# TensorE's instruction order beside a chain of scans: the shared expert's pieces dealt 5 in 8 slots, router and projection queued later

## The reference

```
xc, z = split(x @ W_in.T)                       # 256 + 256
xs = silu(conv3(xc))                            # three taps along time
dt = softplus((xs @ W_x[:64].T) @ W_dt.T + b_dt) + 1e-5
B, Cp = xs @ W_x[64:80].T, xs @ W_x[80:].T      # 16 + 16 per token
s_t = exp(-exp(A_log) * dt_t) * s_(t-1) + B_t * dt_t * xs_t     # state: 256 x 16
y = (Cp @ W_C.T) * sum_n(s_t) + D * xs
layer 1: x1 = x + layernorm((y @ W_out.T) * silu(z)),   fed with layernorm(x)
layer 2, on xn = layernorm(x1):
    router: softmax(xn @ gate_w.T), the best 2 of 8 experts, weights normalised
    routed = sum over the 2 experts of w_e * (gelu(xn @ W1_e + b1_e) @ W2_e + b2_e)   # 256 -> 1024 -> 256
    shared = gelu(xn @ sW1 + sb1) @ sW2 + sb2                                          # 256 -> 1024 -> 256
    out = x1 + layernorm(routed + shared)
```

## Time and profile before

| | us |
|---|---|
| median of 3 runs | 1368.14 |
| the profiled execution | 1368.64 |
| its span, first to last instruction | 1366.8 |
| chunks 0 to 7, first scan to last scan | 47.41 to 632.28 |
| tail to the last router logit | 632.28 to 678.66 |

### The profile page before, as it was taken

The page is one execution under the profiler, slowest core; times in us unless marked ns, Lnnn a source line. Parts: engine busy times, 40 slices in busy tenths (PEclk is TensorE's granted clock), DMA queues, the critical chain, the costliest instruction groups (busy, mean ns, idle before and its releaser), DMA issues.

```text
span 1366.8 us, 14546 instructions
## 1 busy us (share of the span) xinstructions
PE 1142.7 (84%) x4810; PEld 902.0 (66%) x4810; DVE 699.8 (51%) x1201; ACT 625.4 (46%) x1129; POOL 594.5 (43%) x637
## 2 busy tenths in 40 slices
PE   4445597877969697849578999999999999999996
PEld 2112274655637373637577888888888888888874
DVE  1699999899989989895365111111111111111126
ACT  4683977777877887845130221222212222122212
POOL 2594958677695948663001232322323223232111
PEclk9676699897979798878795999999999999999998
DMA  4100102011010101010104365766677656456456
GB/s 136 32 0 0 47 1 75 3 47 31 24 54 24 54 1 62 0 56 7 62 5 161 96 225 174 255 205 226 215 241 247 214 165 221 175 190 214 138 169 200
DMA packets 117835, 152.18 MB, mean 111 GB/s; under 512 B 15206, under 2 KB 102591, under 8 KB 117760
## 3 DMA queue, kind: packets, MB, share of 16 engines
q1 hardware_dynamic: 110272, 132.63, 29.9%
q0 software_dynamic: 7488, 18.63, 3.7%
HBM read 126.06 MB, written 27.00 MB: 112 GB/s over the span
## 4 chain that ended last, share of the span: by engine, by line
PE 58%; DVE 14%; POOL 9%; issue 8%; ACT 8%; DMA 1%; SPq 1%; DVEq 0%; POOLq 0%; ACTq 0%
PE psum L728 20%; PE psum L740 20%; PE psum L672 6%; POOL Ssum L1269 5%; DVE S L907 5%; PE psum L662 2%; PE psum L700 2%; DVE psum L888 2%; PE psum L687 2%; ACT A L1166 2%; DVE stats L843 2%; PE psum L769 1%; PE psum L715 1%; PE psum L642 1%; POOL xs L1243 1%
## 5 line engine op out<-in xcount | busy, mean ns | idle before, releaser
L1208 ACT ACTIVATE h<-psum,bb 128x256 f32<-128x256 f32 x312 | 130.7, 470 | 475.7 <-PE psum L728 444.7
L1269 POOL TENSOR_TENSOR Ssum<-Ssum,S 128x512 f32<-128x512 f32 x240 | 302.3, 1267 | 75.3 <-DVE S L907 75.2
L728 PE MATMUL psum<-XT,w 128*128 128x256 f32 x1248 | 278.8, 382 | 0.9 <-DVE XT L1021 0.9
L740 PE MATMUL psum<-w,h 128*128 128x256 f32 x1248 | 275.8, 379 | 0.0
L728 PEld LDWEIGHTS psum<-XT,w 128*128 128x128 f32 x1248 | 239.1, 192 | 34.4 <-DVE XT L1021 1.3
L740 PEld LDWEIGHTS psum<-w,h 128*128 128x128 f32 x1248 | 234.2, 190 | 30.3
L1294 POOL DMA_INDIRECT z_d<-y,ids x78 | 78.4, 1005 | 390.2 <-DVE y L1029 376.5
L1166 ACT ACTIVATE A<-dts,nea 128x512 f32<-128x512 f32 x256 | 177.3, 720 | 23.0 <-DVE S L907 19.8
L888 DVE TENSOR_TENSOR psum<-us,psum 128x512 f32<-128x512 f32 x256 | 163.6, 683 | 26.2 <-PE psum L628 24.2
L1029 DVE TENSOR_TENSOR y<-bb,psum 128x256 f32<-128x256 f32 x78 | 29.3, 417 | 249.3 <-PE psum L740 249.3
L1021 DVE COPY XT<-psum 128x512 f32<-128x512 f32 x39 | 27.0, 691 | 246.9 <-PE psum L715 240.7
(11 more groups left out here) (153 smaller groups left out, 1196.1 us busy)
## 6 DMA issues: line engine op xcount, KB each, us to landing
w<-W SPq DMA_DIRECT2D x78, 1024.0 KB
Z<-z_d SPq DMA_DIRECT2D x32, 256.0 KB, 6.7
bb<-b SPq DMA_DIRECT2D x39, 128.0 KB
xnb<-x SPq DMA_DIRECT2D x16, 256.0 KB, 3.7
Xr<-x SPq DMA_DIRECT2D x16, 256.0 KB, 3.1
x_d<-gb SPq DMA_DIRECT2D x8, 512.0 KB, 2.9
xn_d<-nb SPq DMA_DIRECT2D x8, 512.0 KB, 3.2
sh_d<-O SPq DMA_DIRECT2D x16, 256.0 KB, 2.5
```

The source lines that it names most:

```text
L728: i = eng.matmul(PS[3 + m % 3][:, 256 * ff:256 * ff + 256], w1[n % 2][:, k, 128 * (f + ff):128 * (f + ff) + 128], xT[n % 2][:, k, :], star ...
L740: i = eng.matmul(PS[6 + n % 2][:, 256 * j:256 * j + 256], h[n % 2][:, f, 128 * j:128 * j + 128], w2[n % 2][:, f, :], start=f == 0, stop=f ...
L1208: eng.activation(h[n % 2][:, f + ff, :], PS[3 + m % 3][:, 256 * ff:256 * ff + 256], ACT.Gelu, bias=bb1[n % 2][:, f + ff:f + ff + 1]).then_ ...
L1269: eng.tensor_tensor(to, to, of, ALU.add).then_inc(nsum, 1)
```

## The change

`shared` is advanced in slots where `5 * k % 8 < 5` only, which are 5 of every 8, instead of in all of them; `post` is stretched over slots 2 to 29 instead of 2 to 27, and gets one more empty step before norm 3 and two between the `nT` copies and `logit`; `prep` gets one more empty step between `silu` and `dtc`. No instruction is added or removed. All lines behind the edits are 6 higher in the changed kernel (628 is 634).

```
-FIRST_POST, LAST_POST, LAST_PREP = 2, 27, 26
+FIRST_POST, LAST_POST, LAST_PREP = 2, 29, 26
...
         say("silu", i)
+        yield
         yield
         yield
         d, p, t0, t1 = (next(use) for _ in range(4))
...
         if not late:
             yield
             yield
+            yield
         yield from normalised(3, i, late)
         say("store_xn", i)
         yield from crossed("nT", i)
+        if not late:
+            yield
+            yield
         g = next(use)
         say("logit", i, g)
...
-            if i:
+
+            if i and 5 * k % 8 < 5:
                 part(beside, 1)
```

## The result

The changed kernel takes 1390.72 us (median of 4 runs, 1390.43 to 1391.23) against 1367.92 for the kernel before in the same comparison: a ratio of 1.0165 with a 95% interval of 1.0147 to 1.0183. It is slower by 22.8 us. The forecast was 1367.3 us, and its range ended at 1377.

What follows compares the result with a forecast made beforehand. DVE was taken to set the pace, its idle waits being winnable. Chunks 2 to 6 +2.1, chunk 1 -4.0, chunk 7 -0.5, tail +1.6: -0.8 on 1368.64, less 0.5 to the median, 1367.3 us; eight-in-ten range 1353 to 1377.

Steps and rivals of the forecast that it cites:

- The gelu block of 5.39 us in front of decay 15: Slot 10's gelu and table loads behind norm 2 delay decays: DVE waits 2.9 us at slot 15, 1.8 at slot 19.
- the late waits behind the logit and the `s1` pieces: DVE's waits for spreads 14 and 15 go, as both spreads now stand ahead of that PE work; part of 21.9 us.
- GpSimd's 4.7 us: DVE's waits for the residual in chunks 2 to 6 go, as it now precedes the second convolution in GpSimd's queue.
- The tail: After the last chunk, `Xr` loads later behind the last `s2_out`, so the residual starts at 667.8 instead of 666.23: +1.6 us.
- Rival 1: Slot 10's gelu is covered by ACT's idling, so no scan waits for a decay: 1345 us, chance 0.14.
- Rival 3: The logit still waits for `nT` copies that come later, so the change fails its purpose: +7, 1375 us, chance 0.08.
- All 21.9 us go.: In chunks 2 to 6, all of `mult`'s waits for spreads, 21.9 us in 20 waits, disappear.
- rival 2: PE's half clock holds through slots 18 to 23 (`dtc`, `s2`, `bp`), making spread 11 late: +15, 1382 us, chance 0.10.
- the size of `gated`'s wait: `gated` of the second half, now behind slot 7 instead of 8, waits for the second `wout`: 0.6 us per chunk.
- the rule on gaps that the prediction weighed: Skill's advice: short matmul bursts with idle gaps fall to half clock, so keep them together; its effect was put as rival 2.
- Chunk 1: No gelu in slot 10 there; -2.3 and -2.3 of waits, plus 0.2 for `gated` and 0.4 for softplus: -4.0 us.
- Softplus: DVE's wait at `dt_sum` for ScalarE's softplus, per chunk: 1.2 us in even chunks, 0.9 in odd ones.

Runs made afterwards that it cites:

- after_s2_less: Changed kernel without two of the four `s2` pieces of every second half (slots 20 and 21): 1378.36 us, ratio 1.0059 to the kernel before.
- after_warm: Changed kernel with 8 extra 128x256 matmuls ahead of `wout` in each chunk: 1379.47 us, ratio 1.0071 to the kernel before.
- thin_only: Kernel before with only the shared pieces thinned to 5 of 8 slots, all else as before: 1380.44 us against 1369.17, ratio 1.0081.

## Why the prediction was wrong

**What held.** That no instruction changes and only waits do. The gelu block of 5.39 us in front of decay 15: 2.9 and 1.8 us were worked out for an even chunk, 3.04 and 1.48 measured, 20.4 us in all against the forecast's 22.5. That the late waits behind the logit and the `s1` pieces go, and GpSimd's 4.7 us. The tail: +1.6 forecast, +1.6 measured, through `Xr` as described, with no gain from the earlier `wout`. Rival 1 is out: the decays weren't covered. Rival 3 is out: the logit held no spread up.

**First failed step: "All 21.9 us go."** The spreads' waits of before go, but 14.0 us come back at spread 12, one in each chunk. The step looked at the spreads near the old waits and, for slots 18 to 23, at spread 11 only, for the half clock of rival 2. It didn't add up the row that follows: `dt`, `s2`, `nT`, `dt`, `s2` from the copy `dcb` on, 6.3 us of PE work (399.93 to 406.20), where a pair of slots leaves 3.5. Before, no `s2` piece stood there. after_s2_less shows it: without two pieces 0.7 us are left. The same step missed spread 8: two `s2` pieces stand in front of it now too (380.46), behind the second half of z, for whose bank PE waits 1.13 us. The 2.0 to 2.3 us that it is late only show where the wait for A is gone.

**Second failed step: the size of `gated`'s wait.** 0.6 us per chunk were forecast, 3.0 in five chunks together, and 14.4 came. The mechanism is the one named; the price was read from a `wout` at the full clock. In the kernel before, pieces kept PE busy until 351.2, 14.0 us into chunk 4; now its last one ends 9.9 us into the chunk, while `wout` comes 14.9 us into it in both. So PE idles 5.02 us and `wout` takes twice as long. after_warm measures this part: 10.3 of the 14.4 us. It is the rule on gaps that the prediction weighed, at a place where it hadn't looked, and it doesn't hold for every gap (chunk 7): `dtc` was at the half clock as before, but `bp` and the pieces behind it at the full one, so rival 2's place and price are both wrong, though its sign and, by chance, its 1382 us came nearer.

**Chunk 1**: -4.0 forecast, -1.35 measured. `gated` waits 1.8, since `wout` takes 3.58 us there; spread 12 is waited for by 1.3 us, and 1.1 for GpSimd's power are new. **Softplus**: 5.4 us forecast, none measured, because the wait for spread 12 comes first and covers it: in after_s2_less, where that wait is gone, 2.3 us of it show.

In sum for chunks 2 to 6: 20.4 + 14.4 + 14.0 = 48.8 us of new waits, against 30.9 forecast, and 28.8 gone as forecast, so +20.0 by these rows. Measured are 19.5 us more of idling, as the small gaps shrank, and 1.8 of busy time, together the 21.3.

## What to carry to other kernels

When work is moved out of a place on an in-order engine, read its idle time there again: what stood in the gap may have kept TensorE's clock up for the next matmul on the path, and a duration from the old trace holds only at the old clock. When work is moved into a place, add up the whole row from the last thing that it waits for to each instruction that another engine needs, not only the first. And waits of the pacing engine don't add: taking out 20.4 us of them gave 6.6, since the next one stood behind.

## What was not expected of the hardware and the kernel

TensorE's `wout` (8 records of 128x256) took 1.97 us after 0.92 us of idling, 1.99 after 1.47, 3.34 after 2.88 and 3.75 after 5.02, all in chunk 4; but 1.97 after 3.19 in chunk 7 of the changed kernel and 3.56 after 2.02 in chunk 5 of thin_only. Eight useless matmuls per chunk made the changed kernel 11.3 us faster. One empty step less in the order of the next chunk's `prep` (after_prep_back) made it 17 us slower; a part of this is the logit, which waits 4.86 us in chunk 4 for a bank that it inherits from `s2_out`, since the PSUM banks are handed on in the order of the list. And DVE's `nm`, 0.14 us by itself, ends together with the GpSimd addition that runs beside it, which makes it up to 1.25 us long in the changed kernel.
